# Attention of a macaron block on one core: the projection to v and router logits, from two fp32 matmuls to six fp32r matmuls on high and low parts

## What is computed

```python
def _L0_attn_ref(X, Wq, Wk, Wv, Wc, Ltri):        # 16 heads of 16, causal
    Q, K, V = (X @ Wq.T), (X @ Wk.T), (X @ Wv.T)   # each reshaped to heads
    KVc = jnp.cumsum(jnp.einsum('blhd,blhe->blhde', K, V), axis=1)
    Y = jnp.einsum('blhd,blhde->blhe', Q, KVc)
    Bm = Lm @ jnp.swapaxes(Lm, -2, -1)             # Lm = lower triangle of Ltri
    Y = jnp.einsum('hed,blhd->blhe', Bm, Y)
    return Y.reshape(Bsz, Lq, Dm) @ Wc.T

x = x + 0.5 * _L0_ffn_ref(_layernorm(x), Wr, W1, W3, W2)   # 8 experts, top 2, capacity 2560
x = x + _L0_attn_ref(_layernorm(x), Wq, Wk, Wv, Wc, Ltri)
x = x + 0.5 * _L0_ffn_ref(_layernorm(x), Wr, W1, W3, W2)
```

## Time and profile before

| what | value |
|---|---|
| time, median of 3 runs | 3151.95 us (3150.39 to 3155.76) |
| the profiled execution's own time | 3149.82 us |
| its span | 3148.1 us |
| PE busy | 2983.8 us (95%) |
| DVE busy | 1454.1 us (46%) |
| ACT busy | 1290.6 us (41%) |
| POOL busy | 1073.6 us (34%) |
| expert stages, in the span | about 170 to 1393 us and 1940 to 3148 us |
| middle stage | about 1411 to 1940 us |

### The profile page before, as it was taken

One profiled execution on the slowest core, in us unless ns is written; L12 is line 12 of the kernel. 1 busy time (PEld: TensorE's weight loads), 2 busy tenths in 40 slices (PEclk: granted clock), 3 DMA queues, 4 the chain that ended last, 5 costly groups with the idle time before them and its releaser, 6 DMA issues. The chain is left out here.

```text
span 3148.1 us, 68785 instructions
## 1 busy us (share of the span) xinstructions
PE 2983.8 (95%) x26142; PEld 2873.9 (91%) x26143; DVE 1454.1 (46%) x3401; ACT 1290.6 (41%) x2586; POOL 1073.6 (34%) x1501
## 2 busy tenths in 40 slices
PE   6769999999999999979999995999999999999998
PEld 6669999999999999977888884999999999999998
DVE  7833434343434434325777775434434343434343
ACT  4633434343434434324555453434434343434343
POOL 3833333434333333330121112343433333333333
PEclk6579999999999999989999997999999999999999
DMA  7432222222323231120111103323223123312211
GB/s 252 141 97 38 64 37 60 41 67 33 68 30 70 35 66 29 32 64 28 42 55 43 55 29 95 67 33 69 40 61 69 31 34 67 69 32 67 34 27 31
DMA packets 144275, 181.29 MB, mean 58 GB/s; under 512 B 13808, under 2 KB 118000, under 8 KB 144176
## 3 DMA queue, kind: packets, MB, share of 16 engines
q0 software_dynamic: 53184, 73.51, 14.6%
q1 hardware_dynamic: 81856, 97.30, 10.0%
q10 hardware_dynamic: 9136, 9.18, 0.9%
HBM read 108.63 MB, written 71.31 MB: 57 GB/s over the span
## 5 line engine op out<-in xcount | busy, mean ns | idle before, releaser
L1051 DVE TENSOR_TENSOR e_hid<-e_ps,e_gate 128x512 f32<-128x512 f32 x540 | 373.2, 691 | 1034.8 <-ACT e_gate L1011 1027.7
L85 PE MATMUL e_ps<-e_xT_hi,e_wb_hi 128*128 128x256 f32 x2176 | 611.5, 281 | 0.0
L87 PE MATMUL e_ps<-e_xT_hi,e_wb_lo 128*128 128x256 f32 x2176 | 611.2, 281 | 0.0
L86 PE MATMUL e_ps<-e_xT_lo,e_wb_hi 128*128 128x256 f32 x2176 | 611.2, 281 | 0.0
L85 PE MATMUL e_ps<-e_xT_hi,c_wa_hi 128*128 128x256 f32 x2144 | 601.6, 281 | 4.4 <-DVE e_xT_lo L1045 3.0
L86 PE MATMUL e_ps<-e_xT_lo,c_wa_hi 128*128 128x256 f32 x2144 | 600.6, 280 | 0.0
L87 PE MATMUL e_ps<-e_xT_hi,c_wa_lo 128*128 128x256 f32 x2144 | 600.3, 280 | 0.0
L1055 DVE TENSOR_TENSOR e_h_lo<-e_hid,e_h_hi 128x512 fp32r<-128x512 f32 x540 | 374.5, 693 | 377.8 <-ACT e_h_hi L1013 298.0
L1011 ACT ACTIVATE e_gate<-e_ps 128x512 f32<-128x512 f32 x540 | 322.7, 598 | 530.7 <-PE e_ps L87 497.5
L1013 ACT ACTIVATE e_h_hi<-e_hid 128x512 fp32r<-128x512 f32 x540 | 342.1, 633 | 421.5 <-DVE e_hid L1051 412.6
L891 POOL DMA_INDIRECT x<-e_yrow,e_y_token x140 | 226.0, 1614 | 551.8 <-ACT e_yrow L1024 528.8
(11 more groups left out here) (261 smaller groups left out, 5565.5 us busy)
## 6 DMA issues: line engine op xcount, KB each, us to landing
raw<-w SPq DMA_DIRECT2D x204, 256.0 KB
normed_rows<-r_xn SPq DMA_DIRECT2D x8, 1056.0 KB, 5.4
normed_rows<-mi_xn SPq DMA_DIRECT2D x8, 1056.0 KB, 4.7
r_xin<-x SPq DMA_DIRECT2D x8, 1024.0 KB, 7.9
x<-r_xin ACTq DMA_DIRECT2D x8, 1024.0 KB, 5.2
mi_x<-x SPq DMA_DIRECT2D x8, 1024.0 KB, 8.2
out<-mi_x SPq DMA_DIRECT2D x8, 1024.0 KB, 5.3
e_xrow<-normed_rows,e_token POOLq DMA_INDIRECT x274
```

Of the source, the lines that this page charges most:

```text
L85: pe.matmul(out, a[0], b[0], start=first, stop=False)
L86: pe.matmul(out, a[0], b[1], start=False, stop=False)
L87: return pe.matmul(out, a[1], b[0], start=False, stop=last)
L1051: dve.tensor_tensor(hid[:, j % 2, :], ps3[j % 2][:], gate[:, j % 2, :], ALU.mult).then_inc(hid_ready, 1)
```

## The change

The projection to v and logits now multiplies high and low parts: `xT` is kept a second time as an fp32r tile `xT_hi` (ACT) and the rest as `xT_lo` (DVE, from PSUM minus the high part), and the weight `wvr` is split once into `wvr_hi` and `wvr_lo`. The product of the low parts is left out. The projections to q and k still read the fp32 tile `xT`. PE waits for `xT_low` behind `project_qk` and ahead of `ranks` and `project_v`, since `xv` may not be overwritten before both parts have been read from it.

```diff
@@ Setup
-            ins = dve.tensor_tensor(k.wvr[:, kk, :], self.raw_vr[:, kk, :], self.pb[:, 0:WV], ALU.subtract)
+            ins = dve.tensor_tensor(self.raw_vr[:, kk, :], self.raw_vr[:, kk, :], self.pb[:, 0:WV], ALU.subtract)
         ins.then_inc(self.centered, 1)
+
+    def split_high(self, act):
+        act.wait_ge(self.centered, 1)
+        act.activation(self.k.wvr[0][:], self.raw_vr[:], ACT.Copy).then_inc(self.w_split, 1)
+
+    def split_low(self, dve):
+        k = self.k
+        dve.wait_ge(self.w_split, 1)
+        dve.tensor_tensor(k.wvr[1][:], self.raw_vr[:], k.wvr[0][:].bitcast(F32), ALU.subtract)
...
@@ route_phase
                     if g == 1:
                         su.keep_heads(act)
+                        su.split_high(act)
...
                     if g == 0:
                         su.center(dve)
+                    if g == 2:
+                        su.split_low(dve)
@@ middle_phase
+        xT_parts = [[m.sb(f"xT_{part}{b}", [P, KD, P], F32R) for part in ("hi", "lo")] for b in range(2)]
...
                 def project_v(n):
                     for kk in range(KD):
-                        ins = pe.matmul(xv[:, 0:WV], xT[n % 2][:, kk, :], k.wvr[:, kk, :],
-                                        start=(kk == 0), stop=(kk == KD - 1))
+                        ins = mm3(pe, xv[:, 0:WV], [t[:, kk, :] for t in xT_parts[n % 2]], [w[:, kk, :] for w in k.wvr],
+                                  kk == 0, kk == KD - 1)
...
                     if chunk(n + 2):
                         project_qk(n + 2)
+                        pe.wait_ge(xT_low, n + 3)
                     if c == 3 and g >= 1:
                         r.ranks(pe, g - 1)
...
                 def keep_x(n):
                     act.wait_ge(xt_made, n + 1)
-                    act.activation(xT[n % 2][:], xv[:, 0:D].rearrange("p (a t) -> p a t", a=KD),
-                                   ACT.Copy).then_inc(xT_ready, 1)
+                    x = xv[:, 0:D].rearrange("p (a t) -> p a t", a=KD)
+                    act.activation(xT[n % 2][:], x, ACT.Copy).then_inc(xT_ready, 1)
+                    act.activation(xT_parts[n % 2][0][:], x, ACT.Copy).then_inc(xT_high, 1)
...
+                def low_x(n):
+                    dve.wait_ge(xT_high, n + 1)
+                    wait(dve, v_made, n - 1)
+                    dve.tensor_tensor(xT_parts[n % 2][1][:], xv[:, 0:D].rearrange("p (a t) -> p a t", a=KD),
+                                      xT_parts[n % 2][0][:].bitcast(F32), ALU.subtract).then_inc(xT_low, 1)
...
                 moments_x1(0)
+                low_x(0)
                 for n in STEPS:
...
                     if chunk(n):
                         add_out(n)
                         stats_x2(n)
+                    if chunk(n + 3):
+                        low_x(n + 3)
                     if c < 4 and 0 <= g < MGS - 1:
                         stats_x1(g + 1, 2 * c)
...
@@ Constants
-        self.wvr = m.sb("wvr", [P, KD, WV])
+        self.wvr = [m.sb("wvr_hi", [P, KD, WV], F32R), m.sb("wvr_lo", [P, KD, WV], F32R)]
```

More of the change, by code:

```diff
@@ L468, in __init__ @@
         self.tri_ready = m.sem("su_tri_ready")
+        self.w_split = m.sem("su_w_split")
         self.bbd_made, self.bbd_ready = m.sem("su_bbd_made"), m.sem("su_bbd_ready")
@@ L582, in heads @@
                 ins = pe.matmul(self.pm[:, a * E:(a + 1) * E], self.wcn[:, kk, a * P:(a + 1) * P],
-                                self.k.wvr[:, kk, D:WV], start=(kk == 0), stop=(kk == KD - 1))
+                                self.raw_vr[:, kk, D:WV], start=(kk == 0), stop=(kk == KD - 1))
         ins.then_inc(self.wcr_made, 1)
@@ L1104, in middle_phase @@
         xT_ready = m.sem("xT_ready")
+        xT_high = m.sem("xT_high")
+        xT_low = m.sem("xT_low")
         qk_made = m.sem("qk_made")
```

## The result

| | before | after |
|---|---|---|
| median, 4 runs each on one chip | 3153.08 us | **3235.01 us** (3234.70 to 3239.00) |
| after / before, 95% interval | | **1.0264** [1.0248, 1.0281] |
| profiled execution's own time | 3149.8 us | 3239.0 us |

The account below looks back on a forecast made before the run. PE was taken to bound the kernel. Waits +53.0 (groups 1 to 6), +5.4 (group 7), +2.2 (start), +0.3 (setup) and +15 (clock) on 3149.8 us, plus 2.1 to the median, gave 3228 us; range about 3203 to 3260.

Parts of the forecast that it names:

- the plain step: Step without routing work ahead of x2 (c = 4): period 7.20 us instead of 7.37, a gain of 0.17.
- the ring: Loop v, scores, mask, state, routing piece, x2, statistics, low part, v over PE and DVE: +53.0 us in groups 1 to 6.
- the clock: PE's granted clock falls at half of the 20 long stalls, 1.5 us each: +15 us, ends 0 and 33.
- Setup: One more ACT copy and DVE subtraction of 528 columns before the stages: +0.3 us, between 0 and 1.5.
- c = 5: Step of a group behind the previous step's moments_x1 chain (4.11 us), which now starts after the low part: 9.89 us.
- v, start to scores: On PE, six fp32r matmuls at 0.117 us replace four fp32 records: 0.78 us instead of 0.98, 0.20 saved per step.
- rival 2: Every one of the 20 stalls drops the clock, some for twice as long: 3246 to 3260 us; chance 0.16.
- rival 1: The waits come as forecast but the clock holds: 3213 us; chance 0.20.
- The start: The middle stage's first v waits for low_x(0) behind moments_x1(0): +2.2 us, from 0.
- Group 7: Last group, where only c = 0 to 4 count: 44.0 us against some 38.7, +5.4.
- Rival 3: DVE's lateness is absorbed since PE reaches v after the low part in all steps: faster, 3140 us; chance 0.04.
- Rival 4: v's 264-column products don't run in one pass, 0.225 us each: +40 us, 3268; chance 0.05.

Follow-up runs that it names:

- e1_low_early: Against the change: DVE makes the low part right behind the state, ahead of routing piece, x2 and statistics; 3166.58 us, 1.0043.
- e4_fp32_wait: Against the change: parts and wait stay, but v comes from two fp32 matmuls with a third weight copy; 3239.2 us, 1.0278.
- e3_no_low: Against the change: no low part made, PE waits for the high part, third product takes it again; 3149.12 us, 0.9987.
- e5_fill: The change plus unread fp32 matmuls on PE in the long stalls behind c = 0, 1 and 5; 3211.52 us, 1.0186.
- e10_on_pool_late: The change with POOL making low parts, its row masks spread, and c = 0 and 1 routing pieces behind x2 and its statistics; 3140.12 us, 0.9967.
- the slip: The change with POOL's row masks spread over c = 3 to 6; by mistake DVE still made 63 low parts; 3236.04 us, 1.0267.
- e2_low_twice: The change with DVE's low-part subtraction done twice, first into a spare tile; 3257.4 us, 1.0343.

## Why the prediction was right, and where its terms were off

**Direction and cause: right.** 3228 was forecast, 3235 measured. PE stalls ahead of v for DVE's `xT_lo`, the plain step gains a little, most of the others lose. `e1_low_early` and `e4_fp32_wait` show the wait's place as the cause.

**Partly luck: how close the number came.** In groups 1 to 6 the ring was sized 5.4 us too long and the clock 7.8 us too cheap, and the two nearly cancel. Within the ring, v was taken 0.12 to 0.15 too short and `x2` to the next v 0.11 to 0.16 too long, in each step on the ring, which cancels as well. And the profiled execution lies 89 us above, not 76: some 10 of these stand ahead of the middle stage and behind its last v, where no term was forecast but Setup's 0.3. Both places differ by several us among the kernels above.

**The sum by steps**, periods from v to v at a clock of 1.00:

| step | forecast | measured | why it differs |
|---|---|---|---|
| plain | 7.20 | 7.23 | v longer, `x2` to v shorter |
| c = 0 | 10.31 | 10.20 to 10.63 | |
| c = 1 | 10.07 | 9.71 to 9.85 | |
| c = 2 | 7.44 | 7.55 | |
| c = 3 | 9.01 | 8.89 | |
| c = 5 | 9.89 | 9.33 in four groups, 9.67 and 9.69 in two | v to mask 3.75 in these four, not 4.15 |
| c = 6 | 7.73 | 7.72 | |
| c = 7 | 9.06 | 8.71 to 9.03 | |

- **v, start to scores: 0.90 to 0.93 us, not 0.78.** The matmuls are 0.12 apart, as forecast. But the scores follow the last one after 0.21 (1681.81 to 1682.02), and the second matmul starts 0.21 to 0.23 after the first (1688.33 to 1688.54, 1681.09 to 1681.32). I had spread the spacing of a running series over the ends of a short one. The 0.20 saved in a step were 0.16 (`e3_no_low`), and only half of that in v. The other half, v's earlier start, was in no term.
- **`x2` to the next v: 1.31 to 1.36 us, not 1.47** (1653.62 to 1654.93, 1686.97 to 1688.33). The low part starts 0.85 after `x2`, where I had taken 1.01 from the chain that stood there before.
- **c = 5: 0.56 too long in four groups, 0.2 in two.** I kept the full 4.11 of the one chain of moments that I had read; here v to mask is 3.75 in four groups and 4.11 in two, so the chain itself varies. It is the largest single error of the ring, some 2.7 us over six groups.
- Together groups 1 to 6 were forecast at 424.2 us without the clock (6 x 70.7), and `e5_fill`, with the clock at 1.00, has 418.8.
- **The clock: +15 forecast, 23 measured.** I had it fall at half of the stalls, for 1.5 us each. It fell 13 times against the 18 stalls of c = 0, 1 and 5 in groups 1 to 6, at 22.8 / 13 = 1.75 us each: behind four of six with c = 0, four of six with c = 1, and five of six with c = 5, although these were 1.9 to 2.2 us and not 2.7. So the truth lies between my case and rival 2 (every stall); rival 1 (none) is excluded. The one fall that I had read from stood at the start of the stage, a thin base: the clock had been at its lower level just before (0.50 from 1412 to 1416).
- **The start: +2.2 us forecast.** v came 7.0 us after the first transposes instead of 4.8, as said; by chunk 2, +1.7 were left. **Group 7**: +5.4 forecast, +7.7 measured, 45.1 us against 37.4. One fall of the clock is in it, and five eighths of a mean group, 38.7, were 1.3 too much for the kernel before. **Setup, ACT's second copy**: nothing seen, as said, beyond what varies from one execution to another.
- **A sign that was wrong**: DVE's idle time ahead of the mask was to be as before or less, and it more than doubled, from 35.7 to 84.6 us in groups 1 to 6. The forecast's own loop asks for that: while v waits for DVE, so do the scores, and DVE waits for them next.
- **Rival 3** (faster, 3140) failed: a group takes 73.6 us, not about 60, and behind every step with c = 0, 1, 3 and 5 of these groups v waits for `xT_lo`. **Rival 4** failed: matmuls of 264 columns start 0.12 us apart.
- In the Trainium skill, "TensorE: Matmul & The Clock Gate", section "HAM oscillation — how this bites in real kernels", the cure for a clock that falls at each wait of a loop is to order the work so that TensorE stays busy. `e5_fill` agrees: the clock held and 23 us came back. The larger part, 47.6 us, needed the wait itself gone. Where that section has the clock fall at every wait, as rival 2 did, this trace has it fall at 13 of 18.

## What to carry to other kernels

Before you move work off the leading engine, find where the helper's new step stands in its own order, and what it depends on there: with one 0.41 us subtraction at the end of DVE's step the change cost 2.6%, with the same subtraction a few lines earlier 0.4%. A wait that closes a ring over two engines turns both engines' slack into time, so mean load says little about it; add up the ring, step by step. When PE's own time has been cut, look for who is waited for next, since the cut is collected only once that is out of the way (`e10_on_pool_late`).

## What the runs showed of the hardware that was not expected

Two stalls of the same size did not do the same to the clock. PE's rows at the two, the first with a fall of the clock behind it and the second without:

```profile
1550.76 0.39 PE L85 MATMUL mi_xv<-c_wvr_hi,mi_xT_hi 128*128 128x264 f32 x1 [1.88 <-DVE mi_xT_lo L1386]
1550.99 0.35 PE L86 MATMUL mi_xv<-c_wvr_lo,mi_xT_hi 128*128 128x264 f32 x1
1551.14 0.42 PE L87 MATMUL mi_xv<-c_wvr_hi,mi_xT_lo 128*128 128x264 f32 x1
1551.36 0.42 PE L85 MATMUL mi_xv<-c_wvr_hi,mi_xT_hi 128*128 128x264 f32 x1
...
1919.69 0.39 PE L85 MATMUL mi_xv<-c_wvr_hi,mi_xT_hi 128*128 128x264 f32 x1 [1.88 <-DVE mi_xT_lo L1386]
1919.91 0.28 PE L86 MATMUL mi_xv<-c_wvr_lo,mi_xT_hi 128*128 128x264 f32 x1
1920.04 0.28 PE L87 MATMUL mi_xv<-c_wvr_hi,mi_xT_lo 128*128 128x264 f32 x1
```

PE was idle for 1.88 us both times. Behind the first the matmuls are soon 0.22 apart (1551.14 to 1551.36), at 1.2 GHz; behind the second they stay at about 0.12. The length of a stall did not decide it either: the stall of 3.18 us shown above, in group 3, kept the clock. So kernels with much the same stalls can differ by several us in the clock alone (6 falls in `e4_fp32_wait`, 11 in the slip, 13 in the change, 14 in `e2_low_twice`), and a forecast of this term needs a range. POOL's subtraction of 128x256 fp32 values in SBUF took 0.73 us, against 0.41 on DVE with one operand in PSUM, so it can serve for a small piece with time to spare. In the Trainium skill, "GPSIMD Engine Reference", section "3.1 Elementwise — side-by-side cycle accounting", a long fp32 `tensor_tensor` add is 1.96 times as slow as on DVE. The ratio here, on a shorter subtraction, is 1.8.
